# Two graph layers over a 6144 x 6144 matrix: other places for the epilogues' loads, six x buffers, and one epilogue product in split parts

## The chip, the cores and the metric

The kernel runs on one core of one Trainium2 chip. The metric is device time in microseconds (us). One launch does the whole computation.

## The reference, cut to what matters

`x` is [6144, 128], `adj` is [6144, 6144], all in float32. Two layers are applied, each followed by a residual and a layer norm, and each multiplies by the whole of `adj`.

```python
# layer 0 (gated)
x_norm = layernorm(x) * g_in + b_in
y_soft = softmax(x_norm @ Wn + bn + gumbel(u))
gate   = (hard + y_soft - y_soft)[:, 1]
view2  = (adj * gate[:, None] * gate[None, :]) @ x_norm
fg     = sigmoid(concat([x_norm, view2]) @ Wg + bg)
fused  = fg * (x_norm @ W1 + b1) + (1 - fg) * (view2 @ W2 + b2)
x1     = layernorm(x + layernorm(fused + x) * g_out + b_out)
# layer 1 (hyperbolic)
xt  = logmap0(proj(mobius_add(mobius_matvec(w_hyp, x1), bias)))
h   = proj(expmap0(relu(logmap0(proj(expmap0(adj @ xt))))))
out = layernorm(x1 + h)
```

## The kernel before, in words

The rows are cut into 12 chunks of 512 rows. The host hands `adj` over as 144 tiles of 1 MB (`A`, ring of five buffers, semaphores `ld0` to `ld4`). Tile (c, q) holds the weights for result chunk c and source chunk q. A product takes 128 columns of the features of chunk q as the stationary operand and 512 columns of a tile as the moving one, and adds up into a bank of PSUM.

**Split products.** Nearly all products are made of three in fp32r (L1030 to L1032): ScalarE copies a half tile into fp32r (`AH`, L563), VectorE subtracts it from the half tile (`AL`, L760), and TensorE adds high x high, high x low and low x high. A half tile is numbered m. A tile used in both layers takes two such sets. The 12 tiles of the first row (c = 0) and a few others go through one plain float32 product instead (L1028), "whole" tiles.

**First pass, row c = 0 (to 79 us).** The features do not exist yet; the loop over k (0 to 11) makes chunk k+2's features while TensorE multiplies chunk k. ScalarE loads `x` chunk by chunk into three buffers `XIN = (XR, FU, GB)` from its own DMA queue (`load_x`, L511). VectorE takes mean and variance (`stats_pre`), GpSimd the power -0.5, ScalarE normalizes (L528), TensorE transposes (L1015), ScalarE copies out with gain and bias (`XNT`, L537, stored to DRAM by `store_xnt`), TensorE makes rows and logits (L1022), VectorE and ScalarE the gate, and ScalarE scales the rows by the gate into `FULL` (L549). TensorE fills waits of the opening with products into an unused bank (`keep_clock`, L1009). All twelve gates are transposed (L1097), copied by ScalarE (L609, semaphore `gate_rows`) and stored to DRAM by SyncE's queue.

**Rows c = 1 to 11.** While row c is multiplied, the layer-0 epilogue of row c-1 ("front") and the hyperbolic part of row c-2 ("back") run between its half tiles. Each engine's program is one list over m, and the tables DVE_FIRST, ACT_FIRST and PE_FIRST say after which half tile of a row each step stands, with one number for c up to 6 (LATE) and one for later rows. The front needs three loads of 256 KB (`load_front`, L349 to L351, semaphore `epi_in`): the gates `GB`, the transposed normalized rows `XNT` and `XR` (the rows of `x`). VectorE multiplies the row's sums by the gates ("gate", L857); TensorE makes the epilogue product ("l0", L1119 to L1127): per block of 128 rows a bias from ones x `BP`, `XNT` x `RX` (L1123, 256 columns, W1 and half of Wg), for fronts 0 to 3 also identity x `XR`, and gated sums x `RS` (L1127). Then tanh, "fuse", two layer norms, the transpose ("tr", L1132) and the hyperbolic product ("mx", L1137) follow.

**Order on SyncE's queue.** SyncE issues all tile loads in order; the load of tile n waits until the splits of tile n-5 are done. `load_front(c)` stands ahead of tile 12c+10, and waits for `l0_mm` and for `v2`, the variance of the second layer norm of the front before it (it frees `XR`). `store_x1(c-2)` stands ahead of tile 12c and waits for `x1_ready`. The gate store stands ahead of tile 16, and ahead of tile 17 stand the waits for its landing and for all stores of `XNT`, with `load_front(0)`.

**Second pass (from about 660 us).** The tiles that layer 1 still lacks are loaded again and multiplied, with the last epilogues between them; nothing of it is touched by the change but the place of two stores.

## Time and profile before

| | us |
|---|---|
| median of 3 runs | 958.48 (958.42 to 961.66) |
| the profiled execution | 959.11 |
| its span | 957.3 |
| PE / DVE / ACT / POOL busy | 916.5 / 788.3 / 679.2 / 228.8 |
| granted TensorE clock, mean | 0.991 |

The times of the rows come from the one profiled execution and count from the start of its span. PE is TensorE, PEld its weight loads, DVE VectorE, ACT ScalarE, POOL GpSimd, SPq and ACTq the instructions with which SyncE and ScalarE issue DMAs. A float32 product shows as two records, an fp32r or bfloat16 product as one.

### The profile page before, as it was taken

The page shows a single profiled execution, that of the slowest core. Times are in us where ns is not written, and L with a number is a line of the kernel's source. Part 1 is how long each engine was busy: PE and PEld are TensorE (multiplying, and loading weights), DVE is VectorE, ACT ScalarE, POOL GpSimd, SP SyncE. Part 2 cuts the span into 40 slices and gives each one's busy share as a digit, 9 for nine tenths or more (in the row PEclk, how much of TensorE's full clock was granted, in tenths as well). Part 3 has the DMA queues.
Part 4 walks back from the last instruction along what each step waited for, and adds up shares of the span by engine and source line. Part 5 has one row for each costly group of instructions (what it writes and reads, how often), then busy time and mean ns, then how long its engine had stood idle before and what let it go on. Part 6 is the DMA issues. An engine that isn't in the chain of part 4 may idle for free.

```text
span 957.3 us, 12597 instructions
## 1 busy us (share of the span) xinstructions
PE 916.5 (96%) x4060; PEld 719.6 (75%) x4060; DVE 788.3 (82%) x1781; ACT 679.2 (71%) x1214; POOL 228.8 (24%) x201
## 2 busy tenths in 40 slices
PE   8898998999999999999999999998899999999993
PEld 4454776877888878888888888886677878778773
DVE  3677789999989799869686785869899898999886
ACT  5675686878767577747566465666778989789873
POOL 2210202111111111101020010111100664484473
PEclk9999999999999999999999999999999999999997
DMA  6988596876959586957666485566799999999980
GB/s 262 357 286 318 211 425 244 342 298 274 361 210 374 196 338 234 331 200 289 234 241 243 177 288 196 203 258 234 271 361 350 420 378 417 371 414 410 396 324 33
DMA packets 51825, 281.72 MB, mean 294 GB/s; under 512 B 6528, under 2 KB 8496, under 8 KB 20656
## 3 DMA queue, kind: packets, MB, share of 16 engines
q1 hardware_dynamic: 46432, 271.48, 74.3%
q10 hardware_dynamic: 5328, 9.44, 2.6%
q8 instruction: 32, 0.52, 0.2%
q14 instruction: 33, 0.27, 0.1%
HBM read 271.44 MB, written 9.46 MB: 293 GB/s over the span
## 4 chain that ended last, share of the span: by engine, by line
PE 65%; DVE 21%; DMA 4%; ACT 4%; POOL 3%; issue 3%; POOLq 0%; SPq 0%; DVEq 0%; ACTq 0%
PE PS L1030 19%; PE PS L1032 19%; PE PS L1031 19%; DVE AL L760 5%; DVE XGL L760 3%; DVE XTL L760 3%; POOL r_rs L456 2%; PE PS L1127 2%; PE PS L1123 2%; PE PS L1028 2%; DMA FU<-in_x_dram 1%; DVE BS L709 1%; DMA A<-in_adjT_dram 1%; ACT FULL L549 1%; PE PS L1137 1%
## 5 line engine op out<-in xcount | busy, mean ns | idle before, releaser
L563 ACT ACTIVATE AH<-A 128x1024 fp32r<-128x1024 f32 x247 | 252.7, 1057 | 114.7 <-PE PS L1032 90.3
L760 DVE TENSOR_TENSOR AL<-A,AH 128x1024 fp32r<-128x1024 f32 x247 | 294.2, 1218 | 38.1 <-ACT AH L563 36.9
L1030 PE MATMUL PS<-AH,XGH 128*128 128x512 f32 x344 | 139.1, 404 | 4.3 <-DVE AL L760 4.2
L760 DVE TENSOR_TENSOR XGL<-A,XGH 128x1024 fp32r<-128x1024 f32 x113 | 132.3, 1216 | 2.5 <-ACT XGH L563 2.4
L1032 PE MATMUL PS<-AH,XGL 128*128 128x512 f32 x344 | 134.2, 390 | 0.0
L1031 PE MATMUL PS<-AL,XGH 128*128 128x512 f32 x344 | 134.0, 389 | 0.0
L563 ACT ACTIVATE XGH<-A 128x1024 fp32r<-128x1024 f32 x113 | 112.8, 1055 | 12.9 <-DMA A<-in_adjT_dram 11.2
L1030 PE MATMUL PS<-AH,XTH 128*128 128x512 f32 x290 | 114.8, 396 | 3.9 <-DVE AL L760 3.9
L1032 PE MATMUL PS<-AH,XTL 128*128 128x512 f32 x290 | 113.0, 389 | 0.0
L1031 PE MATMUL PS<-AL,XTH 128*128 128x512 f32 x290 | 112.9, 389 | 0.0
L456 POOL TENSOR_TENSOR r_rs<-r_v,NHALF 128x4 f32<-128x4 f32 x24 | 44.4, 1848 | 275.9 <-DVE r_v L715 275.9
L760 DVE TENSOR_TENSOR XTL<-A,XTH 128x1024 fp32r<-128x1024 f32 x92 | 108.5, 1218 | 0.4 <-ACT XTH L563 0.3
L563 ACT ACTIVATE XTH<-A 128x1024 fp32r<-128x1024 f32 x92 | 93.2, 1051 | 7.7 <-DMA A<-in_adjT_dram 5.5
L1030 PE MATMUL PS<-XGH,XTH 128*128 128x512 f32 x226 | 90.8, 402 | 4.0 <-DVE XGL L760 4.0
L1032 PE MATMUL PS<-XGH,XTL 128*128 128x512 f32 x226 | 88.1, 390 | 0.0
L1031 PE MATMUL PS<-XGL,XTH 128*128 128x512 f32 x226 | 88.0, 389 | 0.0
L1030 PEld LDWEIGHTS PS<-AH,XGH 128*128 128x128 f32 x344 | 64.7, 188 | 19.2 <-DVE AL L760 4.8
L1032 PEld LDWEIGHTS PS<-AH,XGL 128*128 128x128 f32 x344 | 64.6, 188 | 13.9
L1031 PEld LDWEIGHTS PS<-AL,XGH 128*128 128x128 f32 x344 | 64.7, 188 | 12.9
L1030 PE MATMUL PS<-XTH,XGH 128*128 128x512 f32 x184 | 71.9, 391 | 0.7 <-DVE XTL L760 0.7
L1031 PE MATMUL PS<-XTL,XGH 128*128 128x512 f32 x184 | 71.6, 389 | 0.0
L1032 PE MATMUL PS<-XTH,XGL 128*128 128x512 f32 x184 | 71.6, 389 | 0.0
(250 smaller groups left out, 1564.9 us busy)
## 6 DMA issues: line engine op xcount, KB each, us to landing
A<-in_adjT_dram SPq DMA_DIRECT2D x243, 1024.0 KB, 7.2
GB<-gate_scratch SPq DMA_DIRECT2D x12, 256.0 KB, 3.7
XNT<-xnt_scratch SPq DMA_DIRECT2D x12, 256.0 KB, 4.1
XR<-in_x_dram SPq DMA_DIRECT2D x12, 256.0 KB, 4.8
x_scratch<-X SPq DMA_DIRECT2D x12, 256.0 KB, 7.6
XR<-in_x_dram ACTq DMA_DIRECT2D x4, 256.0 KB, 6.5
FU<-in_x_dram ACTq DMA_DIRECT2D x4, 256.0 KB, 7.1
GB<-in_x_dram ACTq DMA_DIRECT2D x4, 256.0 KB, 6.0
```

Source lines behind the costliest of these rows:

```text
L456: g.tensor_tensor(dst, src, NHALF[:, 0:src.shape[-1]], ALU.pow).then_inc(S[done], 1)
L549: a.activation(whole(k)[:, blk(t)], xcell(k, t)[:, 0:P], ACT.Copy, scale=GATE[:, k * BLK + t:k * BLK + t + 1]).then_inc(S["xgf"], 1)
L563: a.activation(high(m), A[:, n % RING, h * HW:(h + 1) * HW], ACT.Copy).then_inc(S["hi"], 1)
L709: last = v.bn_stats(BS[:, t, :], src[:, blk(t)])
L760: v.tensor_tensor(low(m), A[:, n % RING, h * HW:(h + 1) * HW], high(m).bitcast(F32), ALU.subtract).then_inc(S["lo"], 1)
L1028: return p.matmul(acc, whole(q)[:, blk(t)], A[:, m // 2 % RING, t * CW:(t + 1) * CW], start=start, stop=stop)
L1030: p.matmul(acc, hi[:, st], high(m)[:, mv], start=start, stop=False)
L1031: p.matmul(acc, hi[:, st], low(m)[:, mv], start=False, stop=False)
L1032: return p.matmul(acc, lo[:, st], high(m)[:, mv], start=False, stop=stop)
L1123: p.matmul(E[:, t, 0:2 * P], XNT[:, blk(t)], RX[:, :], start=False, stop=False)
L1127: last = p.matmul(E[:, t, right], GB[:, blk(t)], RS[:, right], start=False, stop=True)
L1137: last = p.matmul(E[:, t, 0:P + 1], X1T[:, blk(t)], RM[:, :], start=True, stop=True)
```

## The change

Four groups of edits.

1. **Six x buffers.** `XIN` gets three more buffers in `PART` (free until row 6), so that six chunks of `x` are loaded at the start; chunk k+6 is loaded where it was. `stats_pre(2)` moves ahead of `neg_mean_pre(1)`, `transposed(0)` ahead of the exponential's table load, and nine keep_clock products become three (after the first sixteen and three).
2. **Gate store and first front load on ScalarE.** ScalarE stores the gates right behind the copy; after the splits of tile 12 it waits for the landing and issues the three loads of front 0. All epilogue steps of row 1 move back by two half tiles (OPENING).
3. **Later places on SyncE's queue.** `load_front(c-1)` stands ahead of tile 12c, `store_x1(c-2)` ahead of tile 12c+3.
4. **Split product.** For fronts 4 to 11 ScalarE copies `XNT` into fp32r ("xnh"), VectorE subtracts ("xnl"), and each float32 product with `RX` becomes three fp32r products of 256 columns. The two parts of `RX` are made once, in the first pass. The new tiles lie where two of `FULL`'s buffers and `BR` were.

```diff
+SPLIT_ROWS = 4
+OPENING = 2
+DVE_FIRST: "xnl": (3, 0)        ACT_FIRST: "xnh": (2, 0)
-        XIN = (XR, FU, GB)
+        XIN = (XR, FU, GB, PART[:, 3, :], PART[:, 4, :], PART[:, 5, :])
...
-                    out.setdefault(2 * NCH * c + after[c > LATE], []).append((event, c))
+                    out.setdefault(2 * NCH * c + after[c > LATE] + (OPENING if c == 1 else 0), []).append((event, c))
...
-                if n == 16:
-                    sp.wait_ge(S["gate_rows"], 1)
-                    sp.dma_start(gate_dram..., GATET[:, :]).then_inc(S["gate_stored"], 16)
-                if n == 17:
-                    sp.wait_ge(S["gate_stored"], 16)
-                    for i in range(3):
-                        sp.wait_ge(S[f"xnt_stored{i}"], 16 * (NCH // 3))
-                    load_front(0)
-                if c >= 2 and c <= NCH + 1 and k == 0:
+                if c >= 2 and c <= NCH + 1 and k == 3:
                     store_x1(c - 2)
-                if 1 <= c < NCH and k == 10:
-                    load_front(c)
+                if 2 <= c <= NCH and k == 0:
+                    load_front(c - 1)
...
 (ScalarE)
-            for k in range(3):
+            for k in range(6):
                 load_x(k)
+            def load_first_front():
+                act.wait_ge(S["gate_stored"], 16)
+                for i in range(3):
+                    act.wait_ge(S[f"xnt_stored{i}"], 16 * (NCH // 3))
+                act.dma_start(GB, ...); act.dma_start(XNT, ...); act.dma_start(XR, ...)
...
+            transposed(0)
             act.wait_ge(S["const"], 1)
             a.activation(JUNK[:, 0:1], NHALF[:, 0:1], ACT.Exp)
-            load_x(3)
-            transposed(0)
...
             a.activation(GATET[:, :], PS[0:NB, 7, 0:P], ACT.Copy).then_inc(S["gate_rows"], 1)
+            act.wait_ge(S["gate_rows"], 1)
+            act.dma_start(gate_dram..., GATET[:, :]).then_inc(S["gate_stored"], 16)
+                if event == "xnh" and front is not None and front >= SPLIT_ROWS:
+                    act.wait_ge(S["epi_in"], 48 * (front + 1))
+                    act.wait_ge(S["l0_mm"], front)
+                    a.activation(XNH[:, :], XNT[:, :], ACT.Copy).then_inc(S["xnh"], 1)
...
                 if m == 2 * NCH + 1:
                     act.wait_ge(S["rm_psum"], 1)
                     a.activation(RM[:, :], PS[:, 4, 0:P + 1], ACT.Copy).then_inc(S["rm_ready"], 1)
+                    load_first_front()
 (VectorE)
+                    link(v.tensor_copy(RXH[:, :], RX[:, :]))
+                    v.tensor_tensor(RXL[:, :], RX[:, :], RXH[:, :].bitcast(F32), ALU.subtract).then_inc(S["bias_ready"], 1)
+                if event == "xnl" and front is not None and front >= SPLIT_ROWS:
+                    dve.wait_ge(S["xnh"], front - SPLIT_ROWS + 1)
+                    v.tensor_tensor(XNL[:, :], XNT[:, :], XNH[:, :].bitcast(F32), ALU.subtract).then_inc(S["xnl"], 1)
 (TensorE)
-            keep_clock(3)
+            keep_clock(1)
             transposes(1)
-            keep_clock(3)
+            keep_clock(2)
             rows_and_logits(1)
-            keep_clock(3)
...
+                    if front >= SPLIT_ROWS:
+                        pe.wait_ge(S["xnl"], front - SPLIT_ROWS + 1)
...
-                        p.matmul(E[:, t, 0:2 * P], XNT[:, blk(t)], RX[:, :], start=False, stop=False)
+                        if front >= SPLIT_ROWS:
+                            p.matmul(E[:, t, 0:2 * P], XNH[:, blk(t)], RXH[:, :], start=False, stop=False)
+                            p.matmul(E[:, t, 0:2 * P], XNL[:, blk(t)], RXH[:, :], start=False, stop=False)
+                            p.matmul(E[:, t, 0:2 * P], XNH[:, blk(t)], RXL[:, :], start=False, stop=False)
+                        else:
+                            p.matmul(E[:, t, 0:2 * P], XNT[:, blk(t)], RX[:, :], start=False, stop=False)
```

## Rows read from the trace of the kernel before

**Rows 1.** The profile's page: busy time of TensorE, and its granted clock in 40 slices
```profile
PE 916.5 (96%) x4060; PEld 719.6 (75%) x4060; DVE 788.3 (82%) x1781; ACT 679.2 (71%) x1214; POOL 228.8 (24%) x201
PEclk9999999999999999999999999999999999999997
```
**Rows 2.** Busy time by stretch: bounds, length, busy us (instructions), clock, DMA share, GB/s
```profile
24.00:28.00 4.00, 2.72 (x9) 0.99 (x7) 1.69 (x12) 1.14 (x3) 0.19 (x1) 1.00 1.01 406
88.00:92.00 4.00, 2.38 (x7) 1.87 (x8) 3.32 (x4) 0.90 (x1) 0.00 (x0) 0.71 1.03 399
100.00:110.00 10.00, 10.00 (x46) 8.29 (x45) 8.72 (x24) 7.85 (x11) 2.60 (x2) 1.00 0.08 32
740.00:760.00 20.00, 20.00 (x91) 16.52 (x91) 17.62 (x17) 19.77 (x51) 11.77 (x13) 1.00 1.02 422
```
**Rows 3.** The timeline of the opening: start, length, instruction, idle before it and its releaser
```profile
8.33 1.28 ACT L580 ACT_TABLE_LOAD   x1
10.90 1.65 ACT L528 ACTIVATE X<-FU,NMP,RSP 128x128 f32<-128x128 f32 x4 [0.41 <-ACT XNT L537]
...
16.86 1.88 PE L1028 MATMUL PS<-A,FULL 128*128 128x512 f32 x4
...
26.10 0.87 DVE L709 BATCH_NORM_STATS2 BS<-FU 128x6 f32<-128x128 f32 x4 [4.18 <-DMA FU<-in_x_dram]
29.09 1.16 PE L1022 MATMUL PS<-IW,XNT 128*128 128x130 f32 x8 [2.37 <-ACT XNT L537]
...
35.75 1.96 PE L1028 MATMUL PS<-A,FULL 128*128 128x512 f32 x4
...
40.85 1.96 PE L1028 MATMUL PS<-A,FULL 128*128 128x512 f32 x4
```
**Rows 4.** The timeline at the first front's loads
```profile
77.11 0.34 SPq L394 DMA_DIRECT2D gate_scratch<-GATET  x1
...
79.03 2.01 ACT L563 ACTIVATE XTH<-A 128x1024 fp32r<-128x1024 f32 x2
81.01 0.33 SPq L349 DMA_DIRECT2D GB<-gate_scratch  x1
...
81.85 0.43 SPq L351 DMA_DIRECT2D XR<-in_x_dram  x1
...
88.68 0.69 DVE L857 TENSOR_TENSOR GB<-PS,GB 128x512 f32<-128x512 f32 x1 [4.85 <-DMA XR<-in_x_dram]
89.62 0.47 PE L1122 MATMUL PS<-BP,ones 128*128 128x384 bf16 x1 [4.47 <-DVE GB L857]
96.86 0.69 PE L1030 MATMUL PS<-AH,XGH 128*128 128x512 f32 x1
```
**Rows 5.** SyncE's own waits: line, releaser, us in total, times, longest
```profile
SPq L250 <- DVE r_v L715: 115.5, 11, 17.8
```
**Rows 6.** The timeline: TensorE's waits in rows 1 to 6
```profile
113.03 0.66 PE L1132 MATMUL PS<-IW,X 128*128 128x128 f32 x4 [0.72 <-ACT X L636]
122.47 0.50 PE L1030 MATMUL PS<-AH,XGH 128*128 128x512 f32 x1 [0.60 <-DVE AL L760]
166.41 0.50 PE L1030 MATMUL PS<-AH,XGH 128*128 128x512 f32 x1 [1.27 <-DVE AL L760]
210.49 0.50 PE L1030 MATMUL PS<-AH,XGH 128*128 128x512 f32 x1 [1.14 <-DVE AL L760]
```
**Rows 7.** Groups by line and shape: busy us and mean ns, then idle before
```profile
L1030 PEld LDWEIGHTS PS<-AH,XGH 128*128 128x128 f32 x344 | 64.7, 188 | 19.2 <-DVE AL L760 4.8 <-issue 1.6
L554 ACT ACTIVATE XGH<-FULL 128x512 fp32r<-128x512 f32 x12 | 7.5, 633 | 0.0
L752 DVE TENSOR_TENSOR XGL<-FULL,XGH 128x512 fp32r<-128x512 f32 x12 | 8.2, 690 | 8.8 <-ACT XGH L554 8.8
```
**Rows 8.** The timeline of TensorE: starts of like products, split and plain
```profile
106.03 0.39 PE L1030 MATMUL PS<-XTH,XGH 128*128 128x512 f32 x1
...
106.71 0.39 PE L1030 MATMUL PS<-XTH,XGH 128*128 128x512 f32 x1
...
211.98 1.05 PE L1137 MATMUL PS<-RM,X1T 128*128 128x129 f32 x8
...
270.44 0.65 PE L1123 MATMUL PS<-RX,XNT 128*128 128x256 f32 x2
270.92 0.59 PE L1127 MATMUL PS<-RS,GB 128*128 128x256 f32 x2
```
**Rows 9.** Waits by pair: VectorE's gate step for TensorE
```profile
DVE GB L857 <- PE PS L1032: 18.9, 6, 5.8
```

More of the change, by code:

```diff
@@ L73 @@
 LATE = 6
+OPENING = 2
 RELOAD_AFTER = 4
 CLOSE = 12
-DVE_FIRST = {"m2m": (6, 1), "part": (7, 3), "gate": (4, 1), "q": (7, 1), "fuse": (10, 6), "stats1": (10, 8),
+DVE_FIRST = {"xnl": (3, 0), "m2m": (6, 1), "part": (7, 3), "gate": (4, 1), "q": (7, 1), "fuse": (10, 6), "stats1": (10, 8),
              "nm1": (11, 9), "resid": (13, 9), "curv0": (14, 4), "affine": (13, 11), "stats2": (13, 11),
@@ L79 @@
              "xtl": (24, 22)}
-ACT_FIRST = {"mx": (3, 1), "tq": (9, 3), "tanh": (10, 6), "y1": (13, 11), "x1": (19, 15), "x1t": (19, 21),
+ACT_FIRST = {"xnh": (2, 0), "mx": (3, 1), "tq": (9, 3), "tanh": (10, 6), "y1": (13, 11), "x1": (19, 15), "x1t": (19, 21),
              "ln": (20, 17), "scale": (23, 21), "xth": (24, 23)}
@@ L145, in build @@
         AL = sb("AL", [P, SPLITS, HW], F32R)
-        FULL = sb("FULL", [P, 3, CW])
+        with nc.sbuf_tensor("FULL", [P, 2, CW], F32) as FULL, nc.sbuf_tensor("BR", [P, CW], BF16) as BR:
+            pass
+        XNH = sb("XNH", [P, CW], F32R)
+        XNL = sb("XNL", [P, CW], F32R)
+        RXL = sb("RXL", [P, 2 * P], F32R)
+        FULL2 = sb("FULL2", [P, CW])
         XGH = sb("XGH", [P, N], F32R)
@@ L165, in build @@
         ident = IW[:, 0:P]
-        RX = sb("RX", [P, 2 * P])
+        RXH = sb("RXH", [P, 2 * P], F32R)
         RS = sb("RS", [P, 3 * P])
@@ L183, in build @@
         WH = PART[:, 1, 0:P]
+        RX = PART[:, 2, 0:2 * P]
         U = sb("U", [P, NB * 2])
@@ L303, in whole @@
         def whole(q):
-            return FULL[:, q % 3, :]
+            return FULL2[:, :] if q % 3 == 2 else FULL[:, q % 3, :]
         def second_features(q):
@@ L509, in load_x @@
             def load_x(k):
-                wait_n(act, "pre_y", BLK * (k - 2))
-                act.dma_start(XIN[k % 3][:, :], x[k * P:(k + 1) * P, :]).then_inc(S[f"xin{k % 3}"], 16)
+                wait_n(act, "pre_y", BLK * (k - 5))
+                act.dma_start(XIN[k % 6][:, :], x[k * P:(k + 1) * P, :]).then_inc(S[f"xin{k % 6}"], 16)
             def store_xnt(k):
@@ L515, in store_xnt @@
                 act.dma_start(xnt_dram[k * P:(k + 1) * P, :], XNTB[k % 3][:, :]).then_inc(S[f"xnt_stored{k % 3}"], 16)
-            for k in range(3):
+            for k in range(6):
                 load_x(k)
+            def load_first_front():
+                act.wait_ge(S["gate_stored"], 16)
+                for i in range(3):
+                    act.wait_ge(S[f"xnt_stored{i}"], 16 * (NCH // 3))
+                act.dma_start(GB[:, :], gate_dram[0:1, :].partition_broadcast(P)).then_inc(S["epi_in"], 16)
+                act.dma_start(XNT[:, :], xnt_dram[0:P, :]).then_inc(S["epi_in"], 16)
+                act.dma_start(XR[:, :], x[0:P, :]).then_inc(S["epi_in"], 16)
             def gumbel_ln(i):
@@ L527, in normalize @@
                 for t in range(BLK):
-                    a.activation(YB[k % 2][:, blk(t)], XIN[k % 3][:, blk(t)], ACT.Identity,
+                    a.activation(YB[k % 2][:, blk(t)], XIN[k % 6][:, blk(t)], ACT.Identity,
                                  bias=NMP[:, k % 3, t:t + 1], scale=RSP[:, k % 3, t:t + 1]).then_inc(S["pre_y"], 1)
@@ L721, in stats_pre @@
             def stats_pre(k):
-                dve.wait_ge(S[f"xin{k % 3}"], 16 * (k // 3 + 1))
+                dve.wait_ge(S[f"xin{k % 6}"], 16 * (k // 6 + 1))
                 wait_n(dve, "pre_rs", k - 2)
-                stats(XIN[k % 3], MVP[:, k % 3, :, :], VP[:, k % 3, :], "pre_v")
+                stats(XIN[k % 6], MVP[:, k % 3, :, :], VP[:, k % 3, :], "pre_v")
             def neg_mean_pre(k):
@@ L780, in prepare @@
                 if k == 10:
[L781 removed]
+                    link(v.tensor_copy(BP[64:65, :], B4[64:65, :]))
+                    link(v.tensor_copy(RXH[:, :], RX[:, :]))
+                    v.tensor_tensor(RXL[:, :], RX[:, :], RXH[:, :].bitcast(F32), ALU.subtract).then_inc(S["bias_ready"], 1)
             stats_pre(0)
@@ L789, in _ @@
             stats_pre(1)
+            stats_pre(2)
             neg_mean_pre(1)
@@ L795, in _ @@
                                    op0=ALU.mult, op1=ALU.add).then_inc(S["gumbel"], 1)
-            stats_pre(2)
             dve.wait_ge(S["gumbel"], 1)
```

10 lines of the change are left out of this document (3 added, 7 removed).

## Prediction, made before the changed kernel ran

> **What bounds the kernel now.** I read the page first. TensorE is busy 96% of the span at full clock in all but the last slice [rows 1]; no other engine is near that. So two kinds of time can be won: what TensorE idles, and what its own products cost. Then came TensorE's timeline, gap by gap. Of 41 us of idle time (957.3 less 916.5) about 13 lie behind its last big product at 942 us and 8 in the second pass's start (664 to 726 us); the change touches neither. The rest is the opening, one hole at the first epilogue, and small waits in rows 1 to 6. Windows over these stretches say what is missing there [rows 2]: in 24 to 28 us TensorE is busy 2.72 of 4 us while the DMA engines are full; in 88 to 92 us its granted clock is 0.71, a mix of 2.4 and 1.2 GHz; in 100 to 110 us the DMA engines move 32 GB/s, hence SyncE is held up. SyncE's own waits name the holder: `load_front` waited 115.5 us in 11 times for the variance that frees `XR` [rows 5].
>
> All sums are made against the profiled execution, 959.11 us (span 957.3 and 1.8 around it). It is 0.6 us above the median of the runs, which I take off at the end.
>
> **Opening.** TensorE's period per chunk, once it runs, is 40.85 - 35.75 = 5.10 us, and it is busy all through it [rows 3]. Its first product is at 16.86, the fourth chunk's (k = 3) at 35.75. At three periods it would be at 16.86 + 15.3 = 32.2, so 3.6 us were lost between. The cause is the wait of VectorE for the fifth `x` (buffer `FU`, 4.18 us, landed at 26.1), which comes out on TensorE as 2.37 us before the rows of chunk 3 [rows 3] and smaller waits about it. With six buffers that `x` is asked for at about 3 us and the wait goes: 3.6 us.
>
> The first product itself moves too. ScalarE's `normalize(1)` at 10.90 stood behind the table load (8.33, 1.28 long) [rows 3] and the copy of `XNT(0)`, 0.76. The order of the two is swapped, so `normalize(1)` stays at about 10.9 to 12.6. Behind it TensorE had keep_clock products in its way; of those ahead of the first product, nine become three. Nine took 3 to 4.5 us of a queue that ran at the lower clock about 10.6 to 14 us, not all of it on the path. By the chain (normalize to 12.6, transposes to 12.8, copy to 13.7, rows and logits to 14.9) the first product is at about 15.0 to 15.4, 1.5 us to 1.9 us earlier. I take 1.5. Three more issues of 0.45 us on ScalarE's queue end at 3.6 us, ahead of the first table load, which must end before 5.24: 3.6 + 1.28 = 4.9, hidden, without much to spare. `stats_pre(2)` ahead of `neg_mean_pre(1)` costs at most 1.6 us of VectorE and lies beside the table load. Total 5.1 us. Bounds: 0, if the tiles of `adj` take the place of `x` as what is late; 7, with the chain at its shortest. I take the working value, since the wait has its own row.
>
> The Trainium skill (DMA: Bandwidth & Descriptors, Issuing engines are not separate DMA queues) says that transfers begun by different engines run on the same 16 DMA engines and interleave. So the three extra `x` (0.79 MB) do not come free: they delay tiles 0 and 1. The trace shows a common limit, DMA share 1.01 at 406 GB/s in 24 to 28 us [rows 2]. 0.79 MB at that rate are 1.9 us; how late tiles or small vectors can then be is rival A.
>
> **First front's loads.** Before, TensorE began the split products at 79.4, did four half tiles (27 at most by its place), and sat 4.47 us until 89.62, for the gated sums, and these for `XR`, issued at 81.85 and in use at 88.68 [rows 4]. The first products behind the hole ran at half clock: clock 0.71 over 4 us is 58% of them at 1.2 GHz, and with the slices behind it about 3.4 us, worth 1.7 us. The half tile after the epilogue started at 96.86, so half tile 30 at 96.86 + 2 x 1.36 = 99.6. A half tile is six products, and three take 106.71 - 106.03 = 0.68 us [rows 8].
>
> After, ScalarE issues the gate store at about 77.3, where SyncE did at 77.11; it landed 3.9 us on, as SyncE's next issue at 81.01 shows [rows 4]. ScalarE has done two half tiles by 79.0, and now stands still to 81.1, then issues three loads at 0.43 each, to 82.4. That is the wait which the change adds: behind it stand the splits of half tile 26 on, and so VectorE and TensorE. Copy (1.06) and subtraction (1.22) put half tile 26 on TensorE at 84.7, where it would be 82.15: 2.5 us idle. Cover from there: TensorE does 26 to 29 to 90.1; the loads, issued 81.1 to 82.4, take up to the same 6.8 us and land by 89.2; VectorE is through its split of half tile 30 at about 89.2 and the gate at 89.9. So the product starts at 90.1 without a hole and takes 5.85 us at full clock: half tile 30 at 95.95. Gain 99.6 - 95.95 = 3.6 us. A hole of 2.37 us at 26.7 left the clock at 1.00 [rows 2, 3], so I put no clock loss on the new one. Bounds: 0 (loads later and a clock loss of 1.7), 5.5 (no stall).
>
> **Loads on SyncE's queue.** Ahead of tile 12c+10 the wait for `v2` came two half tiles and 2 us of statistics too late for that tile; ahead of tile 12c that tile needs half tile 24c-9 anyway, which is where `v2` is due. The three front loads still have eleven half tiles (15 us and more) for their 7. `store_x1` three tiles later no longer waits. What that is worth on TensorE's path is bounded by its waits there: eight in rows 1 to 6, 6.6 us together, of which [rows 6] has four. Two of them (0.60 and 1.27) stand behind a ScalarE that had waited 2.9 and 3.7 us for a tile; the one at 210.49 has a 2.0 us tile wait but also VectorE's own chain before it; 113.03 is VectorE's epilogue chain. I take 2.5 us, with 0 and 6 as bounds. From row 7 on TensorE has no gap, and nothing can be won.
>
> **The split product.** 8 fronts x 4 blocks = 32 products. A split product of 512 columns takes 0.68 / 3 = 0.227, so 256 columns 0.113, and with a fixed part 0.12; three are 0.36. The float32 product takes four passes, 4 x 0.113 = 0.45 (0.48 from its start to the next one's) [rows 8]. 32 x 0.09 = 2.9 us won. Bound above: if a weight load of 0.188 [rows 7] is not hidden behind a stream this short, three take 0.56, and 32 x 0.11 = 3.6 us are lost. Eight float32 records of 129 columns, two passes each, take 1.05 us with the last one's tail [rows 8], 0.13 each at most with a new weight load every time; that is the nearest row and speaks for hidden. Bound below: 0.11 each against 0.48, 4.8 us won.
>
> The new copy (0.633) and subtraction (0.690) [rows 7], eight times each, are 5.1 us of ScalarE and 5.5 us of VectorE. From row 7 on VectorE waits for TensorE ahead of the gate (18.9 us in 6 times [rows 9]), right behind the new step: hidden. In rows 5 and 6 VectorE has little to spare; I put 0.5 us (0 to 1.4). Making the parts of `RX` costs VectorE about 0.7 us once at about 75 us, ahead of a wait for ScalarE: nothing.
>
> **Sum.** 5.1 + 3.6 + 2.5 + 2.9 - 0.5 = 13.6 us; 959.1 - 13.6 = 945.5, and on the scale of the median 944.9. I say 945.
>
> **Rivals.**
> A: the opening is held by tiles or the small vectors instead, behind six `x` loads. For: the DMA engines are full by 20 us. Against: they were not in 12 to 20 us. The opening then gives 5.1 - 1.9 = 3.2 or less, say 2: 948.
> B: ScalarE's stall at the gate store is longer, and the clock falls behind the new hole. For: every piece of that chain is a latency. Against: the hole of 2.37 us. The first front gives 0: 948.5.
> C: the waits of rows 1 to 6 nearly all go, since VectorE in rows 2 and 3 inherits each hold-up from tiles. 2.5 becomes 6, and the opening 6: 940.5.
> D: no change that can be told: the second pass runs with full DMA engines (share 1.02, 422 GB/s in 740 to 760 us [rows 2]), and takes back what the first gave, as tiles come at their own rate. Against: TensorE is busy 20.00 of 20 us there, and tiles are asked for as buffers come free, so the stream moves along. 957.
> E: slower: an fp32r product of 256 columns runs at a float32 product's pace (0.45). Then 3 x 0.45 - 0.45 = 0.9, 32 times 28.8 us lost for 10.7 won elsewhere: 977. It decides above 0.26 us a product. Against: 512 columns take 0.227.
>
> **Numbers.** My forecast 0.56, A 0.12, B 0.12, C 0.12, D 0.05, E 0.03. Range 939 to 953: it takes in A, B, C and single bounds. A measurement here tells 0.5% (4.8 us) from no change. Faster by more than that: forecast and A to C, 0.92; same 0.05; slower 0.03.
>
> **What would show it.** The fourth chunk's product at about 30.5 us; the one hole at the start of row 1 of about 2.5 us, with the clock at 1.00; SyncE's wait for the variance down from 115 us to some 20; the split products 0.12 us apart; no new TensorE gap ahead of the epilogue products from front 4 on. It would be wrong if the hole in row 1 grows past 4 us, if the first product doesn't come before 16 us, or if gaps come up in rows 5 to 12.

## The result, and the profile after

The changed kernel takes 953.21 us (median of 6 runs, 950.17 to 954.52), the kernel before 959.05 us on the same chip (6 runs, 957.98 to 961.66). The ratio is 0.9933 [0.9921, 0.9944]: 0.7% faster, less than half of what was forecast. The profiled execution of the changed kernel took 953.25 us, with a span of 951.0 us, 6.3 us less than before. Its page, the row of busy times that answers to [rows 1] (the clock's row is unchanged):

```profile
PE 912.3 (96%) x4086; PEld 718.2 (76%) x4086; DVE 793.5 (83%) x1791; ACT 682.2 (72%) x1222; POOL 232.8 (24%) x201
```

TensorE lost 4.2 us of busy time; VectorE and ScalarE gained 5.2 and 3.0 (the new subtractions and copies). The page can't say where the other 2 us came from, nor where the missing 7 went. For that I set the start of like products side by side in both timelines (us from the start of the span):

| TensorE starts | before | after | ahead by |
|---|---|---|---|
| first product | 16.86 | 14.69 | 2.2 |
| chunk k = 3 | 35.75 | 30.05 | 5.7 |
| chunk k = 4 | 40.85 | 36.37 | 4.5 |
| chunk k = 8 | 61.27 | 58.03 | 3.2 |
| last plain product | 77.32 | 74.07 | 3.3 |
| first split product | 79.43 | 76.70 | 2.7 |
| half tile 31 | 101.27 | 96.50 | 4.8 |
| l0 of front 1 | 133.06 | 127.65 | 5.4 |
| l0 of front 3 | 221.07 | 215.84 | 5.2 |
| l0 of front 6 | 361.47 | 355.70 | 5.8 |
| l0 of front 11 | 648.98 | 641.57 | 7.4 |
| last product | 943.29 | 936.71 | 6.6 |

The forecast's own landmark, chunk 3 at about 30.5, is met. Three microseconds are given back between 30 and 77 us: 1.2 at each of two waits for `x`, and 0.5 ahead of the first split product. There TensorE waits 0.67 us where it waited 0.15 before, because ScalarE now issues the gate store (73.87 below) ahead of its copy of tile 12, and is idle for 0.40 us there. That half microsecond belongs to part 2.

The 2.2 us at the first product are not all the edit's. In the profile of before TensorE ran at half clock from 11.0 to 14.5 us. In another profile with the same opening (part 3 alone, below) it did not, and the first product stood at 15.52.

The timeline of the opening after, beside [rows 3] (start, length, instruction, idle before it and its releaser):

```profile
14.69 1.88 PE L1044 MATMUL PS<-A,FULL 128*128 128x512 f32 x4
...
18.43 0.79 ACTq L510 DMA_DIRECT2D XR<-in_x_dram  x1
...
25.18 1.98 PE L1044 MATMUL PS<-A,FULL 128*128 128x512 f32 x4 [0.79 <-DMA A<-in_adjT_dram]
...
30.05 1.45 PE L1044 MATMUL PS<-A,FULL 128*128 128x512 f32 x3
31.83 0.87 DVE L720 BATCH_NORM_STATS2 BS<-XR 128x6 f32<-128x128 f32 x4 [3.89 <-DMA XR<-in_x_dram]
34.81 1.16 PE L1038 MATMUL PS<-IW,HY 128*128 128x130 f32 x8 [0.73 <-ACT HY L544]
36.37 1.53 PE L1044 MATMUL PS<-A,FULL 128*128 128x512 f32 x3 [0.39 <-ACT FULL L556]
...
53.43 0.87 DVE L720 BATCH_NORM_STATS2 BS<-PART 128x6 f32<-128x128 f32 x4 [2.28 <-DMA PART<-in_x_dram]
56.69 1.16 PE L1038 MATMUL PS<-IW,XNT 128*128 128x130 f32 x8 [0.74 <-ACT XNT L544]
```

The wait of 4.18 us for the fifth `x` is gone, and a wait of 3.89 us for the seventh has come. It is the first `x` that goes through a buffer twice, asked for at 18.43 while the tile loads fill the DMA engines, and it is in use 13.4 us later. The eleventh waits 2.28 us too.

The first front after, beside [rows 4]:

```profile
73.87 0.33 ACTq L615 DMA_DIRECT2D gate_scratch<-GATET  x1
...
76.70 0.47 PE L1046 MATMUL PS<-XTH,XGH 128*128 128x512 f32 x1 [0.67 <-DVE XTL L771]
...
78.28 0.34 ACTq L523 DMA_DIRECT2D GB<-gate_scratch  x1
79.14 0.45 ACTq L525 DMA_DIRECT2D XR<-in_x_dram  x1
79.64 2.00 ACT L570 ACTIVATE XTH<-A 128x1024 fp32r<-128x1024 f32 x2 [3.23 <-issue]
82.10 0.47 PE L1046 MATMUL PS<-XTH,XGH 128*128 128x512 f32 x1 [2.40 <-DVE XTL L771]
...
86.74 0.69 DVE L873 TENSOR_TENSOR GB<-PS,GB 128x512 f32<-128x512 f32 x1 [0.24 <-DMA XR<-in_x_dram]
...
89.26 0.34 PE L1139 MATMUL PS<-BP,ones 128*128 128x384 bf16 x1
94.83 0.68 PE L1046 MATMUL PS<-AH,XGH 128*128 128x512 f32 x1
```

The 4.47 us hole ahead of the epilogue is gone, and in its place ScalarE's stand at the gate store puts a hole of 2.40 us ahead of half tile 26. The length was worked out as 2.5. Behind it, however, the clock falls. The windows view of that stretch, of one 580 us later, and of the stretches of [rows 2] (bounds, length, busy us of PE, PEld, DVE, ACT, POOL, clock, DMA share, GB/s):

```profile
24.00:28.00 4.00, 3.21 (x14) 1.77 (x13) 2.45 (x14) 2.80 (x10) 2.03 (x4) 1.00 1.03 415
83.30:86.70 3.40, 3.40 (x9) 2.65 (x8) 3.19 (x3) 3.40 (x5) 0.00 (x0) 0.50 1.01 329
663.60:667.00 3.40, 3.40 (x10) 2.62 (x9) 3.33 (x8) 2.65 (x6) 0.37 (x1) 0.50 0.49 149
740.00:760.00 20.00, 20.00 (x94) 16.57 (x93) 17.87 (x28) 18.77 (x46) 14.69 (x18) 1.00 1.00 390
```

A clock of 0.50 for 3.40 us of full work is 1.2 in place of 2.4 GHz and costs 1.7 us. The profile of before has two such stretches (from 11.0 and from 89.7 us), that of after has two (from 83.3 and from 663.4).

SyncE's own waits, which [rows 5] gave as 115.5 us, and TensorE's gaps in rows 1 to 6, beside [rows 6]:

```profile
SPq L257 <- DVE r_v L726: 23.2, 6, 6.6
```
```profile
111.25 0.44 PE L1154 MATMUL PS<-IW,X 128*128 128x128 f32 x2 [0.92 <-ACT X L646]
...
161.19 0.50 PE L1046 MATMUL PS<-AH,XGH 128*128 128x512 f32 x1 [1.63 <-DVE AL L771]
...
205.28 0.50 PE L1046 MATMUL PS<-AH,XGH 128*128 128x512 f32 x1 [1.13 <-DVE AL L771]
...
332.42 0.47 PE L1046 MATMUL PS<-AH,XGH 128*128 128x512 f32 x1 [1.20 <-DVE AL L771]
...
658.07 0.47 PE L1046 MATMUL PS<-AH,XTH 128*128 128x512 f32 x1 [1.39 <-DVE AL L771]
663.25 0.47 PE L1046 MATMUL PS<-AH,XTH 128*128 128x512 f32 x1 [2.22 <-DVE AL L771]
```

SyncE waits 92 us less, and TensorE's gaps are nearly the same ones: they name VectorE's subtraction and the epilogue chain, not a tile. Last, the split product in front 4, beside [rows 8], its copy and subtraction by shape (line, x count, busy us, mean ns, idle before), and VectorE's wait ahead of the gate, beside [rows 9]:

```profile
264.09 0.36 PE L1141 MATMUL PS<-RXH,XNH 128*128 128x256 f32 x1
264.29 0.28 PE L1142 MATMUL PS<-RXH,XNL 128*128 128x256 f32 x1
264.41 0.28 PE L1143 MATMUL PS<-RXL,XNH 128*128 128x256 f32 x1
264.53 0.59 PE L1149 MATMUL PS<-RS,GB 128*128 128x256 f32 x2
```
```profile
L622 ACT ACTIVATE XNH<-XNT 128x512 fp32r<-128x512 f32 x8 | 4.9, 615 | 0.0
L869 DVE TENSOR_TENSOR XNL<-XNT,XNH 128x512 fp32r<-128x512 f32 x8 | 5.5, 685 | 0.0
...
DVE GB L873 <- PE PS L1048: 16.9, 6, 5.2
```

The second and third record are 0.12 us long to the next start, as forecast; the first takes 0.20. A whole block of the epilogue product takes 1.01 us in place of 1.08 to 1.09, so a split product saves 0.08 us. VectorE still waits 16.9 us at the gate in 6 times: the new steps are hidden in the later rows.

### The profile page after: what moved, and what is told of

The parts are those of the page before. It is cut to its first block, busy times and chain, and to the rows that moved or that the text cites. A ratio compares the mean times of both kernels' runs of the same rounds, so it can differ in the third digit from the quotient of the medians.

```text
span 951.0 us, 12683 instructions
## 1 busy us (share of the span) xinstructions
PE 912.3 (96%) x4086; PEld 718.2 (76%) x4086; DVE 793.5 (83%) x1791; ACT 682.2 (72%) x1222; POOL 232.8 (24%) x201
## 4 chain that ended last, share of the span: by engine, by line
PE 59%; DVE 23%; POOL 5%; ACT 5%; DMA 4%; issue 3%; POOLq 0%; ACTq 0%; DVEq 0%
PE PS L1046 17%; PE PS L1048 17%; PE PS L1047 17%; DVE AL L771 5%; DVE XGL L771 5%; DVE XTL L771 3%; POOL r_rs L455 2%; PE PS L1149 2%; DVE BS L720 2%; DMA XR<-in_x_dram 2%; PE PS L1044 1%; DMA PART<-in_x_dram 1%; DMA A<-in_adjT_dram 1%; PE PS L1159 1%; DVE MV L724 1%
## 5 line engine op out<-in xcount | busy, mean ns | idle before, releaser
L1046 PE MATMUL PS<-AH,XTH 128*128 128x512 f32 x290 | 115.0, 397 | 4.2 <-DVE AL L771 4.2
```

Of the source, the lines that this page charges most:

```text
L1046: p.matmul(acc, hi[:, st], high(m)[:, mv], start=start, stop=False)
```

## The experiments

Each kernel was timed on a chip beside the kernel before; ratios are to that one. "After" is the changed kernel. The kernels of one round share a chip; from round to round I compare ratios, not times.

### One part undone at a time

**The changed kernel again, on the chip of the second round.**

> The changed kernel itself, on the chip of the next three, to compare them with it: about 0.993 of the kernel before. Both theories expect the same of it.

954.50 us (10 runs, 952.59 to 958.40), 0.9948 [0.9932, 0.9965]. The two intervals overlap in 0.9932 to 0.9944. In the traces of the two, the landmarks stand up to 2.6 us apart (first split product 76.70 and 77.71, last product 936.71 and 939.32), so a difference under some 2 us between two profiles says nothing by its landmark alone; the gap that makes it must be seen.

**Old opening**: three x buffers and the old order, parts 2 to 4 kept.

```diff
-        XIN = (XR, FU, GB, PART[:, 3, :], PART[:, 4, :], PART[:, 5, :])
+        XIN = (XR, FU, GB)
...
-            keep_clock(1)
+            keep_clock(3)
```

> Changed kernel with part 1 undone: three x buffers, the old order of the opening and the old keep_clock products; parts 2 to 4 stay. Theory (the opening's gain is mostly given back by two late x loads): the first split product comes 2.7 us later than in the changed kernel (79.4 instead of 76.7), and the whole takes 2.7 us longer, about 956. Rival (the opening kept its 5.1 us and something later lost it): 958 or more. In the trace: first product at 16.9, the fourth chunk's at 35.8.

955.80 us, 0.9945 [0.9932, 0.9958]. The first split product is at 80.01, 3.3 us later than after (76.70), and the k = 3 product at 37.09 in place of 30.05, 1.7 of it a stretch at half clock at 30.4. Those 1.7 us are made up later: chunk 8 begins at 61.34, and in before at 61.27. The times put the whole of part 1 at 0.1% or less (0.9945 against 0.9933 and 0.9948), and can't tell it from nothing; the traces put it at 2.3 to 3.3 us at the first split product, against 5.1 forecast.

**First front's loads back on SyncE's queue** (part 2 undone).

```diff
-OPENING = 2
+OPENING = 0
...
+                if n == 16:
+                    sp.wait_ge(S["gate_rows"], 1)
+                    sp.dma_start(gate_dram..., GATET[:, :])...
+                if n == 17:
+                    sp.wait_ge(S["gate_stored"], 16)
+                    load_front(0)
...
-                    load_first_front()
```

> Changed kernel with part 2 undone: gate store and first front load on SyncE's queue, ahead of tiles 16 and 17, and no shift of row 1; parts 1, 3 and 4 stay. Theory (the new hole of 2.4 us and the 3.4 us at half clock behind it eat half of this part's gain of 4.5 + 1.7): 2 to 2.7 us slower than the changed kernel, about 955.5. Rival (the part gives the forecast 3.6 or more): 957. In the trace: a hole of about 4.5 us ahead of the first epilogue product.

953.05 us, 0.9920 [0.9907, 0.9933]: the times do not tell part 2 from nothing. The hole of before is back (4.44 us ahead of the epilogue, half clock behind it), and the wait ahead of the first split product is 0.15 us again. l0 of front 3 is at 217.20 in place of 215.84, 1.4 us later; but 0.7 of that stands already at the last plain product (74.80 in place of 74.07), which part 2 doesn't touch. Counted from there, part 2 is worth 1.5 us at half tile 31, and 0.6 at l0 of fronts 2 and 3, not 3.6. It moved one hole to another place and made it shorter, the clock loss came along, and the wait for ScalarE's `X` in row 2 is 1.16 us with it (at 150.06) and 0.79 without.

**Old places on SyncE's queue** (part 3 undone, parts 1, 2 and 4 kept).

```diff
-                if 2 <= c <= NCH and k == 0:
-                    load_front(c - 1)
+                if 1 <= c < NCH and k == 10:
+                    load_front(c)
```

> Changed kernel with part 3 undone: load_front(c) ahead of tile 12c+10 and store_x1 ahead of tile 12c; parts 1, 2 and 4 stay. Theory (VectorE's own epilogue chain makes TensorE's waits in rows 1 to 6, not late tiles): 0.3 to 0.8 us slower than the changed kernel, about 953.7, with the same gaps of 1.1 to 1.6 us near 160, 204 and 331. Rival (my forecast: the places are worth 2.5 us): 955.7, and SyncE waits over 100 us for the variance again in both.

963.65 us (12 runs), 1.0033 [1.0022, 1.0045]: slower than before. Both theories missed that. The timeline of this kernel in row 1:

```profile
107.78 0.43 SPq L358 DMA_DIRECT2D XR<-in_x_dram  x1
108.25 0.90 SPq L351 DMA_DIRECT2D A<-in_adjT_dram  x2
115.43 2.00 ACT L570 ACTIVATE AH<-A 128x1024 fp32r<-128x1024 f32 x2 [9.03 <-DMA A<-in_adjT_dram]
119.03 1.11 PE L1154 MATMUL PS<-IW,X 128*128 128x128 f32 x4 [9.20 <-ACT X L646]
```

`load_front(1)` waits for the second layer norm's variance of front 0, and tile 22 stands behind that wait on SyncE's queue. Part 2 has moved all of row 1's epilogue back by two half tiles. So the variance comes 0.8 us later, counted from the last plain product, and ScalarE's step `x1`, which stood behind half tile 43, now stands behind half tile 45, the second of tile 22. ScalarE waits 9.03 us for tile 22 with `x1` queued behind, and TensorE's transpose waits 9.20 us for that step, with 6.8 us at half clock around it (115.0 to 121.8). Part 2 is only bearable with part 3.

**Part 3 alone on the kernel before.**

```diff
-                if c >= 2 and c <= NCH + 1 and k == 0:
+                if c >= 2 and c <= NCH + 1 and k == 3:
                     store_x1(c - 2)
-                if 1 <= c < NCH and k == 10:
-                    load_front(c)
+                if 2 <= c <= NCH and k == 0:
+                    load_front(c - 1)
```

> The kernel before with part 3 alone (load_front(c-1) ahead of tile 12c, store_x1 ahead of tile 12c+3). Theory (VectorE's chain, not late tiles, makes the waits in rows 2 to 6): the gap of 0.6 at 121.9 goes, those near 154, 165, 209 and 337 stay, 0.5 to 1.2 us faster than the kernel before. Forecast's view: 2.5 us faster.

958.42 us (7 runs), 0.9978 [0.9967, 0.9989], some 2.1 us. In the trace one gap of [rows 6] has gone (that at 122.47); five others stand, at 0.70 to 1.30 us. From the last plain product to l0 of front 3 it takes 141.36 us, and before took 143.75: 2.4 us less. So part 3 is worth nearly the 2.5 us of the forecast where it stands alone, and in the changed kernel its worth is mostly that it undoes what part 2 would cost.

**The product in float32 again** (part 4 undone, its copies too).

```diff
-                            p.matmul(E[:, t, 0:2 * P], XNH[:, blk(t)], RXH[:, :], start=False, stop=False)
-                            p.matmul(E[:, t, 0:2 * P], XNL[:, blk(t)], RXH[:, :], start=False, stop=False)
-                            p.matmul(E[:, t, 0:2 * P], XNH[:, blk(t)], RXL[:, :], start=False, stop=False)
+                        p.matmul(E[:, t, 0:2 * P], XNT[:, blk(t)], RX[:, :], start=False, stop=False)
```

> Changed kernel with part 4 undone: the epilogue's product of the transposed rows stays one float32 product for all fronts, without the new copy and subtraction; RX has a buffer of its own. Theory (32 products won 0.08 us each, the copies hidden): 2.6 us slower than the changed kernel, about 955.9, the mx steps of rows 5 to 12 falling behind by 0.33 us a row. Rival (the copies on ScalarE and VectorE cost as much as the product gives): within 0.7 us of the changed kernel, 953.2.

954.81 us, 0.9939 [0.9925, 0.9953]. From l0 of front 4 on each front loses 0.31 us against after, 2.2 to 2.6 us over eight. The forecast had 2.9.

### The loads of x

**Early x**: the seventh to ninth `x` are asked for right behind normalize(0) to normalize(2), which free their buffers, and x(k+9) in the loop.

```diff
             normalize(0)
+            load_x(6)
...
-                if k + 6 < NCH:
-                    load_x(k + 6)
+                if k + 9 < NCH:
+                    load_x(k + 9)
```

> Changed kernel with x chunks 6, 7 and 8 asked for right behind normalize(0), (1) and (2), which free their buffers, and chunk k+9 in step k of the loop instead of k+6. Theory (chunks 6 and 10 are asked for late, into DMA engines filled by tile loads, 13.4 us to landing): VectorE's waits of 3.89 and 2.28 us go, the first split product comes at 74.3 instead of 76.7, 2.4 us faster than the changed kernel. Rival (the DMA engines' rate bounds the opening, tiles then come late): tile waits of TensorE in the place of them, less than 1 us faster.

951.31 us, 0.9907 [0.9891, 0.9923], on the chip where after took 954.50. VectorE's waits for `x` are gone, and the first split product is at 74.14, 2.6 to 3.6 us sooner than in the two profiles of after. TensorE's wait for the tile of chunk 2 has grown (1.43 us, and 0.79 and 1.12 in the two of after): the rival's mechanism is there too, but smaller. The seventh `x` is asked for at 8.19, ahead of the crowd:

```profile
8.19 0.37 ACTq L510 DMA_DIRECT2D XR<-in_x_dram  x1
...
29.06 0.86 DVE L723 BATCH_NORM_STATS2 BS<-XR 128x6 f32<-128x128 f32 x4
```

**Tile loads cut to rows of 2 KB.** A tile load takes 128 rows of 8 KB in one DMA, an `x` load 128 rows of 2 KB. Here the first 24 tiles are loaded by four DMAs of 512 columns each, with the same bytes; everything else is the changed kernel.

```diff
-                sp.dma_start(A[:, n % RING, :], adjT[row:row + P, :])...
+                if n < 24:
+                    for i in range(4):
+                        sp.dma_start(A[:, n % RING, i * CW:(i + 1) * CW],
+                                     adjT[row:row + P, i * CW:(i + 1) * CW])...
```

> The changed kernel with each of the first 24 tile loads issued as four DMAs of 512 columns, so that their rows are 2 KB instead of 8 KB; nothing else differs. One look, for the landing of x chunk 6, asked for at about 18.4 us. Theory (the queues share the DMA engines row by row, and 2 KB rows against 8 KB rows get a fifth): x 6 lands within 6 us instead of 13.4, and VectorE's wait of 3.89 us goes. Rival (the x load stands behind a backlog in time, whatever its row size): 12 us or more again.

One run, 949.5 us. The `x` asked for at 18.56 is in use at 27.98, without a wait, where after had 31.83 and a wait of 3.89:

```profile
18.56 0.58 ACTq L519 DMA_DIRECT2D XR<-in_x_dram  x1
27.98 0.86 DVE L729 BATCH_NORM_STATS2 BS<-XR 128x6 f32<-128x128 f32 x4
```

Beside it, the two kernels' small loads and stores (KB each, median us from issue to landing), after first, then this one:

```profile
PART<-in_x_dram ACTq DMA_DIRECT2D x6, 256.0 KB, 9.8
xnt_scratch<-X1T ACTq DMA_DIRECT2D x4, 256.0 KB, 8.6
```
```profile
PART<-in_x_dram ACTq DMA_DIRECT2D x6, 256.0 KB, 6.7
xnt_scratch<-X1T ACTq DMA_DIRECT2D x4, 256.0 KB, 5.8
A<-in_adjT_dram SPq DMA_DIRECT2D x96, 256.0 KB, 6.6
```

With rows of one size these loads of 256 KB take the same 6 to 7 us on either queue. Not every load follows: the one asked for at 18.56 still took 9.3 us (13.4 in after), where the expectation had 6, and that of `XR` for the first front 8.6 us (7.5 in after). The Trainium skill (DMA: Bandwidth & Descriptors, Queues, rings and completion order) says that a DMA engine goes round the queues and drains one packet of several descriptors from a queue before it turns to the next. By that rule a queue with four times the bytes in a row gets up to four times the bytes in a turn; these rows agree with it, though the share itself was not measured. The edit also makes four issues of each tile load, some 0.4 us or more apart, and no run tells that from the size of the rows.

**The same kernel, timed.**

> The kernel small_rows, timed. Theory: 3.2 us faster than the changed kernel by the start of the split products (73.5 against 76.7), so 0.991 of the kernel before. Rival (2 KB rows cost DMA time that comes back later): 0.994 as the changed kernel.

949.18 us (4 runs, 948.01 to 950.56), 0.9893 [0.9880, 0.9906]. With this one edit the kernel is faster than after: its interval stands wholly below both of after's (0.9921 to 0.9944 and 0.9932 to 0.9965).

### The first front

**Late front**: ScalarE issues the three loads two half tiles later, when the gate store has surely landed, to take away the 2.40 us hole.

```diff
                 if m == 2 * NCH + 1:
...
-                    load_first_front()
+                if m == 2 * NCH + 3:
+                    load_first_front()
```

> Changed kernel with ScalarE's wait for the gates' landing and the three loads of front 0 moved behind the splits of tile 13 (m = 27) from behind those of tile 12 (m = 25). Theory (the wait of 2.0 us fits the two splits, so the loads are issued at the same 78.3): the hole of 2.4 us at 79.7 goes, and with it the 3.4 us at half clock at 83.3 (1.7 us), the product starts at 85.5 to 86 instead of 89.26: 3 to 4 us faster than the changed kernel. Rival (the loads' landing takes the hole's place, since XR landed at 86.5): the product starts at 87 to 88, 1 to 2 us faster.

958.58 us (12 runs), 0.9988 [0.9976, 1.0001]: slower than after by 4 us, where a gain was expected.

```profile
79.56 0.45 ACTq L525 DMA_DIRECT2D XR<-in_x_dram  x1
93.75 0.69 DVE L874 TENSOR_TENSOR GB<-PS,GB 128x512 f32<-128x512 f32 x1 [9.10 <-DMA XR<-in_x_dram]
94.69 0.48 PE L1140 MATMUL PS<-BP,ones 128*128 128x384 bf16 x1 [8.62 <-DVE GB L874]
```

`XR` is in use 14.2 us after its issue, against 7.6 in after (79.14 to 86.74). I read it so: in after ScalarE stands still ahead of these loads, so in that time it frees no tile buffer, and SyncE asks for no further tile. Without the stand tile loads run beside them. The issues in the traces agree: behind the issue of `XR` SyncE asks for its next two tiles at 83.11 and 85.38 in after, and at 80.92 and 83.55 in late front. The clock adds to it: late front's profile is at half clock from 89.4 to 99.6, which costs 2.5 us in the 4.9 in which TensorE works.

**Late front with 2 KB rows**, to try that reading: the edits of late front and of the 2 KB rows together.

> The kernel late_front (front 0's three loads behind the splits of tile 13), with the first 24 tile loads in 2 KB rows. Theory (share by row size): the three loads land within 7 us instead of 14, the hole ahead of the epilogue product falls from 8.6 us to under 2, no stretch at half clock; with the x waits gone too, 948 or less, 9 us faster than late_front. Rival (the hole is the backlog of tile bytes): 6 us of hole or more stay.

951.24 us, 0.9914 [0.9900, 0.9928]:

```profile
76.59 0.77 ACTq L534 DMA_DIRECT2D XR<-in_x_dram  x1
86.19 0.69 DVE L883 TENSOR_TENSOR GB<-PS,GB 128x512 f32<-128x512 f32 x1 [4.21 <-DMA XR<-in_x_dram]
87.13 0.48 PE L1149 MATMUL PS<-BP,ones 128*128 128x384 bf16 x1 [4.30 <-DVE GB L883]
```

9.6 us from issue to use in place of 14.2, and 0.7% better than late front: the way the tiles are cut makes much of the difference and not all. Of some 7 us, 3.7 stand already at the first split product (73.93, and 77.63 in late front), where the waits for `x` are gone. A hole of 4.30 us remains.

**Front's loads apart**: early x, and of the three loads only `GB`, which alone needs the gate store, stands behind the wait; `XR` is loaded in step 8 of the first pass and `XNT` ahead of the copy of the gates.

```diff
+                if k == NCH - 4:
+                    act.dma_start(XR[:, :], x[0:P, :])...
...
+            act.dma_start(XNT[:, :], xnt_dram[0:P, :])...
             a.activation(GATET[:, :], PS[0:NB, 7, 0:P], ACT.Copy)...
```

> The early x loads of the run before, and two of front 0's three loads taken out of the place behind the gates: XR is asked for in step 8 of the first pass, XNT ahead of the gates' copy, both free of the gates; only GB stays behind the wait at m = 25. Theory (small loads on ScalarE's queue starve behind tile loads, so fewer of them late is less wait): ScalarE stands 0.9 us less, the hole at row 1 is 1.5 to 1.7 us instead of 2.4, and 1 to 2.7 us are won on early_x (with or without the stretch at half clock): 948.5 to 950. Rival (the hole is the gates' landing alone, the issues don't matter): hole as before, same time as early_x.

950.73 us (946.92 to 951.59), 0.9890 [0.9874, 0.9906]. The epilogue begins at 84.39 (89.26 in after) without a hole ahead of it; the hole ahead of half tile 26 is 1.88 us long, and this profile has no half-clock stretch there. Against early x alone (0.9907 [0.9891, 0.9923]) the intervals overlap, so the times don't show the gain.

**The same with `GB` two half tiles later.**

```diff
-                if m == 2 * NCH + 1:
+                if m == 2 * NCH + 3:
                     load_first_front()
```

> As the kernel beside it, but GB's load moved behind the splits of tile 13 (m = 27). Theory (of the 14.2 us that the three loads took to land in late_front, one alone takes a third to a half, 5 to 7 us): GB, issued at about 75.5, is there by 81 to 83, ahead of the product at 83; no hole over 0.5 us at the start of row 1, no stretch at half clock: 3 to 4 us faster than early_x, 947. Rival (any load that meets the tile loads waits for their backlog, 14 us whatever its size): a hole of 6 us or more as in late_front, slower than early_x.

950.30 us, 0.9893 [0.9876, 0.9910]: no better. ScalarE's stand is gone, and the epilogue waits for `GB` instead:

```profile
76.35 0.34 ACTq L523 DMA_DIRECT2D GB<-gate_scratch  x1
84.84 0.69 DVE L881 TENSOR_TENSOR GB<-PS,GB 128x512 f32<-128x512 f32 x1 [3.50 <-DMA GB<-gate_scratch]
85.78 0.48 PE L1147 MATMUL PS<-BP,ones 128*128 128x384 bf16 x1 [3.25 <-DVE GB L881]
```

Even one load, asked for beside running tile loads, takes 8.5 us. Every version tried has a hole at the start of row 1, ahead of half tile 26 or of the epilogue, from 1.88 us in front's loads apart to 8.62 in late front. What they have in common is the way of the gates through DRAM: store, landing, load. That it is the cause was not tried, as no run took it out.

### Rows 1 to 6, and the edits together

**ln one half tile later** (ln and k at 21 in place of 20, for rows up to 6), to give VectorE room where [rows 6] has its gaps.

```diff
-"ln": (20, 17)     "k": (20, 19)
+"ln": (21, 17)     "k": (21, 19)
```

> Changed kernel with ln and k one half tile later in rows up to 6 (21 in place of 20). Theory (the waits near 160, 204 and 331 are ScalarE's, which stands at ln for VectorE's tc with a split behind it): these three gaps (1.6, 1.1 and 1.2 us) shrink to under 0.5 each, 2 to 3 us faster than the changed kernel. Rival (VectorE as a whole is short of time in these rows): the gaps move one half tile on and keep their sum, no faster.

952.46 us, 0.9925 [0.9909, 0.9942]. Of the gaps, 1.63 became 0.51 and 1.13 became 0.52, and the time from l0 of front 1 to that of front 6 fell only from 227.98 us (in after on this chip) to 227.38. The loss was mostly moved, and the times (after on this chip: 0.9948 [0.9932, 0.9965]) don't tell the two kernels apart. The gaps belong to VectorE's load in these rows, not to a place on SyncE's queue.

**Early x, front apart and late, 2 KB rows**, and **the same with ln later**: the diffs shown above together.

> All of the repairs: early x loads, XR and XNT of front 0 ahead of the gates, GB behind the splits of tile 13, first 24 tile loads in 2 KB rows. Theory: no hole over 0.7 us between 26 us and the first epilogue product, which starts at 81 to 82; 4 us faster than front_apart, 946 to 947 where before is 960.5. Rival (the rate of the DMA engines is the bound, repairs only move waits): 950 as the others.

> The kernel beside it with ln and k one half tile later in rows up to 6. Theory: another 0.6 us as in late_ln, within what the runs can tell. Rival: the same time as without.

950.78 us, 0.9906 [0.9882, 0.9931], and 948.80 us (946.40 to 952.05), 0.9890 [0.9873, 0.9908], on the chip where the 2 KB rows alone took 949.18. The gains do not add: early x and the smaller rows take away the same waits, and the later place of `GB` leaves a hole of 2.1 us in the one and 3.1 in the other. In the profile of the second TensorE also waits 2.21 us for the tile of chunk 2, with 3.4 us at half clock behind it. The second expectation's mechanism, the later ln, can't be told in the times.

## Why the prediction was wrong

The steps that failed are these. The opening and the first front's loads had the right mechanism and the wrong size. The step on SyncE's queue took a wait that was not on TensorE's path. The second pass was put at nothing. Only the split product came as forecast. By the traces of before and after, from landmark to landmark:

| step | forecast | measured |
|---|---|---|
| opening | 5.1 | 3.25 (last plain product) |
| gate store and first front's loads | 3.6 | 1.52 (half tile 31: 4.77, less 3.25) |
| places on SyncE's queue | 2.5 | 0.34 (l0 of front 6: 5.77, less 4.77 and two split fronts of 0.33) |
| split product | 2.9 | 2.64 (eight fronts of 0.33) |
| copies and subtractions | -0.5 | -0.01 (l0 of front 6 to front 11: 1.64, less 5 x 0.33) |
| from l0 of front 11 to the end | 0 | -1.44 |
| sum | 13.6 | 6.30 |

This is one pair of profiles. In the second profile of after the first two rows are 2.25 and 0.11 us, and the sum is 3.7: the small terms are not known better than to 1 or 2 us, but in neither profile do the opening and the first front together (8.7 forecast) reach 5 us.

1. **Opening: a term that was mis-sized.** The prediction followed one wait, that for the fifth `x`, to its end, and it ended: k = 3 at 30.05 against about 30.5. It did not ask the same of the loads left behind. "With six buffers that `x` is asked for at about 3 us and the wait goes" is true of chunks 3 to 5 and says nothing of 6 to 11, which are asked for beside tile loads. Two waits of 3.89 and 2.28 us gave back 2.5 us of the 3 (the other 0.5 is part 2's). Early x shows it: with them asked for sooner, the waits and 2.6 us are gone. The 2 KB rows point to a cause behind: the bytes are the same and the wait is gone, so it may be the share that a queue of short rows gets beside one of long rows; that share was not measured. Rival A had the price (2 to 3.2 us for the opening) and another mechanism: tiles and vectors late behind the `x`. A tile was late once, by 0.79 us; `x` late behind tiles was the larger part.

   The working itself had a misreading: 5.10 us a chunk was taken as TensorE's own period. Chunks follow by 4.77 us where `x` is early (k = 3 to 6 in early x, from 31.18 to 45.48), and after a late chunk 3 in the kernels with the old opening too (part 3 alone: 37.32 to 42.08). So a loss ahead of chunk 3 is partly made up afterwards, and what is won there is partly not kept: part 3 alone has chunk 3 at 37.32, 1.6 us behind before, and its last plain product at 77.64, 0.3 behind.

2. **First front: the hole was foreseen, the clock was not.** 2.40 us against 2.5 computed; the step "A hole of 2.37 us at 26.7 left the clock at 1.00 [rows 2, 3], so I put no clock loss on the new one" fell. It rested on one hole in one profile. Of the eleven profiles of the study with a hole of 1.9 to 2.9 us at the start of row 1, eight had a half-clock stretch behind or in it. That is Rival B's second half, at 1.7 us. The second term left out is the gate store on ScalarE, put at nothing, which cost 0.5 us ahead of tile 12. 3.6 - 1.7 - 0.5 = 1.4 us, and half tile 31 gives 1.5, in the table and against the kernel with the part undone alike. Against that kernel, 0.6 of it is left at l0 of front 2.

   Rivals A and B were priced one at a time, each with the other's part whole. Both came: 13.6 less A's 3.1 and B's 3.6 is 6.9 us, near the 6.3 of the profiles.

3. **SyncE's queue: a wait on a queue was read as TensorE's.** SyncE's wait fell to 23.2 us (some 20 forecast), and TensorE kept its gaps. The prediction itself noted that the gap at 210.49 had VectorE's chain before it. A gap whose releaser is VectorE's subtraction, behind an epilogue step on VectorE, was not cured here by an earlier tile. Late ln moved these gaps by moving VectorE's work, which the queue's places did not. Alone on the kernel before, part 3 gives 2.1 us by the times; what it gives here is tied to part 2, and the prediction did not see that tie (9.20 us if left out). For the same reason rival C could not come about.

4. **Split product: right**, in place (0.12 us apart, but for 0.20 behind the first of the three), in size (0.33 us in a front between after and before, 0.31 against the plain product; 0.08 a product where 0.09 was forecast), and in what hides its copies. Rival E falls: 0.12 us, where it needed over 0.26.

5. **The second pass: put at nothing, cost 1.4 us.** The gaps at 658.07 and 663.25 are VectorE's and were there before (1.06 and 2.21 us, now 1.39 and 2.22). Behind the second the clock falls now (1.7 us) and did not in the profile of before; a gap of 0.68 us at 823.76 is new, and the gaps up to 725 us are 0.9 us shorter in all. That adds up to about the 1.4. None of it follows from the edits as far as a run shows: of the eighteen profiles of this study eight have a half-clock stretch there, between 658 and 673 us, one of them of part 3 alone. Rival D said that the second pass would take back gains because the DMA engines are full. In 740 to 760 us TensorE is busy 20.00 of 20 us before and after, so that mechanism is not seen there. In six other profiles TensorE waits once for a tile, 0.5 to 1.0 us, between 889 and 931 us.

None of the three signs that were to prove the prediction wrong came up: the hole stayed under 4 us, the first product came before 16 us, rows 5 to 12 have no new gaps. The signs stopped at 30 us for the opening, and the loss began at 31.

What stays open: whether the stretch at half clock can be kept away, as it comes in one profile and not in another of like holes; the runs of after go from 950.17 us (mean clock 0.994) to 954.52 us (0.990), which is about the size of two such stretches. And the forecast's 945 us was reached by no version: the best median is 948.80.

## What to carry to other kernels

When more buffers remove a wait at the start, follow every later load of the same stream to the moment it is asked for, and to what else is on the DMA engines then: the wait comes back at the first buffer that is used twice. A small load beside large ones can be late out of proportion to its bytes (13.4 us here); ask for it early, or try the large transfers in rows of the same size. And a wait that stands on an issuing queue is worth on the path only what the last releaser of TensorE's gaps says: read the gaps' releasers first, and look at what a step moved on one engine does to the waits that stand on another queue.

## What the runs showed of the hardware

- A load of 256 KB in 2 KB rows took 13.4 us beside tile loads in 8 KB rows, and 14.2 us at worst (late front); with the tiles in 2 KB rows it took 9.6 us at the place of the 14.2, and the medians fell from 9.8 to 6.7 us (loads into `PART`).
- Gaps of 1.9 to 2.9 us ahead of half tile 26 or of the first epilogue came with 3.4 us or 6.8 us at 1.2 GHz in eight of eleven profiles. Gaps of 2.05, 1.88 and 2.54 us did not, nor did that of 2.37 in the opening of before. So the length of one gap does not settle it within this range. The same opening, in the profile of part 3 alone, had a gap of 4.63 us and 6.8 us at 1.2 GHz.
- fp32r products of 256 columns followed each other by 0.12 us with a new stationary operand each time, so a weight load of 0.19 us did not show behind a product of 0.12; behind the first of the three, which follows a bfloat16 product, the next start was 0.20 us off. The float32 product of the same size takes 0.48 us to the start of the next [rows 8]. By whole blocks of the epilogue product (1.01 and 1.08 to 1.09 us) three split ones were 0.08 us shorter than one plain.
